# Dense work of a finished block, one turn of 16 tiles later in the three relation passes

## The chip, the cores and the metric
The kernel runs on one core of one Trainium2 chip. The metric is the device time of one execution in microseconds, without a profiler. The kernel before took 6027.67 us (median of 3 runs, 6023.32 to 6033.74).

## The reference
Four graph layers act on 5000 nodes with 128 features and 80,000 edges, sorted by target. Each layer normalises the rows (mean and variance over the features, then relu), computes a graph convolution and adds its result to the rows. The first is an attention layer, the second a weighted sum, the third three averaging convolutions. The change touches the fourth, which is three relational convolutions in a row (widths 128 to 256, 256 to 256, 256 to 128), with 8 kinds of edge:

```
seg = dst * 8 + etype
agg = segment_sum(x[src], seg)                 # one sum for each target and kind
mean = agg / maximum(count of seg, 1)
out = einsum('nrd,rdo->no', mean, W) + x @ root + b
h = relu(conv1(x)); h = relu(conv2(h)); out = conv3(h)
```

## The kernel before
Nodes lie in 40 blocks of 128, edges in 625 tiles of 128. A relational convolution is computed the other way round: first each node's row is multiplied with all 8 relation matrices and stored as a table with 8 rows per node; then a pass over the edges gathers for each edge the one row that belongs to its source and kind, weights it, and sums it into its target. The three edge passes are called p5, p6 and p7. While a pass sums, blocks of target nodes become finished one after the other, since edges are sorted by target. The dense work on a finished block (relu, the root product of the next convolution, the products for the next table, copies, the store) is placed between the tiles of the same pass. In p7 the dense work is only a transpose back to rows, the addition of the old rows and the store of the output.

An edge pass works like this. GpSimd gathers one tile after another with indirect DMAs into a ring of 16 slots (`gather`, L925 to L946). Before it fills a slot again, it waits for `mm_done`, which TensorE raises at the end of each quad of 4 tiles. TensorE (`tile`, L2354) multiplies each gathered tile with a selection matrix of 64 columns that VectorE makes; the four tiles of a quad add up in one PSUM bank, of which four are used in turn. VectorE (`quad`, L1781) makes a selection two quads ahead, waits for `mm_done`, adds the bank into the 64-column window of the accumulator, and raises `psum_free`, which frees the bank and also tells how many quads have been added.

Sixteen tiles, that is 4 quads, are a turn (`TURN`); a pass has 39 turns and one last tile. Each engine runs the same list of turns (`turns`, L415). Within a turn, `dense_step` (L426) puts one dense step behind each tile: the first four positions carry steps 12 to 15 of the block that was begun in the turn before, the other twelve carry steps 0 to 11 of the next block. Block b is begun at position 4 of turn b + 1. ScalarE begins it (step 0: `hidden`, L1304, or the copy at L1330): it waits until `psum_free` shows `added` quads, which is all quads up to the first one of the current turn. TensorE's root product is step 2, at position 6, and waits for ScalarE (`hid_made`). Its four table units are steps 4, 7, 10 and 13 in p5 (4 and 7 in p6), and ScalarE copies each from PSUM two steps behind, at 6, 9, 12 and 15, into a buffer that SyncE stores. In p7 TensorE's step 2 is the transpose (L2669) and VectorE's step 7 the sum with the old rows (L2217); SyncE stores the result and then loads the old rows of the block two further on into the buffer that has come free.

The engines' instruction lists are written out in this order; nothing is planned at run time. After the last turn and the last quad, `remaining` (L433) does what is left of the blocks: steps 12 to 15 of block 37, and blocks 38 and 39. The gather of the next pass waits until the tables of all 40 blocks have been stored.

Of the kernel before, what the change touches and what calls it, by code (L numbers as in the profile page):

```python
# [35 lines left out]
BLOCKS = -(-N // P)  # L36
# [14 lines left out]
TURN = 16  # L51
# [3 lines left out]
QUAD = 4  # L55
# [3 lines left out]
CREDIT = 4  # L59
TURNS = T // TURN  # L60
LAG = 2
SLACK = 4
SPAN = 16
SPANS = NP // SPAN
# [24 lines left out]
def build(nc, a, out):  # L89
    ctx = ExitStack()  # L90
    with ctx:
# [5 lines left out]
        def sem(name):  # L97
            if name not in made:
                made[name] = ctx.enter_context(nc.semaphore(name))
            return made[name]  # L100
# [263 lines left out]
        def chunks(p):  # L364
            return PASS[p]["F"] // P
# [37 lines left out]
        def later(i):  # L403
            return not isinstance(i, int) or i > 0
# [10 lines left out]
        def turns(eng, turn):  # L415

            turn(0, None, None, 0, 0)
            turn(1, None, (0, 0, 0), 0, 0)
            pairs = (TURNS - LAG) // 2
            with eng.Fori(0, pairs) as r:  # L420
                turn(2 * r + LAG, (2 * r, 0, r), (2 * r + 1, 1, r), 0, r)
                turn(2 * r + LAG + 1, (2 * r + 1, 1, r), (2 * r + 2, 0, r + 1), 1, r)
            for b in range(2 * pairs, TURNS - LAG):
                turn(b + LAG, (b, b % 2, b // 2), (b + 1, (b + 1) % 2, (b + 1) // 2), b % 2, b // 2)

        def dense_step(dense, j, k, last, first, added):  # L426

            if j < SLACK and last is not None:
                dense(TURN - SLACK + j, k, *last, added)
            if j >= SLACK and first is not None:  # L430
                dense(j - SLACK, k, *first, added)

        def remaining(step):  # L433

            for b in range(TURNS - LAG, BLOCKS):
                for j in range(TURN - SLACK if b == TURNS - LAG else 0, TURN):
                    step(j, b, b % 2, b // 2)

        def block_pairs(eng, body):
# [428 lines left out]
        def _(pool):  # L868
            pool.memset(X[:, (BLOCKS - 1) * P:NP], 0.0).then_inc(sem("x_padded"), 1)
            pool.memset(BASEF[:, :], float(N)).then_inc(sem("x_padded"), 1)  # L870
            pool.memset(HIGHF, 0.0).then_inc(sem("x_padded"), 1)
            pool.memset(TILEF[:, 0:SLACK], 0.0).then_inc(sem("x_padded"), 1)
            pool.iota(TILEF[:, SLACK:SLACK + TP - TURN].rearrange("o (g e) -> o g e", e=TURN), [[P, TP // TURN - 1], [0, TURN]], base=0, channel_multiplier=0,
# [158 lines left out]
        def _(act):  # L1032
# [31 lines left out]
            def dense_steps(p, dense):  # L1064

                with act.Fori(0, km) as k:
                    kq = act.snap((km * ORD[p] + k) * QUADS)

                    def spans(i, x):
                        v = SPAN_SLOT[x]  # L1070
                        span_out(act.snap(k * EARLY + PER_TURN * i + x), PER_TURN * i + x, v,
                                 act.snap(k * (TURNS * SLOT_USES[v]) + SLOT_USES[v] * i + x // 3))

                    def turn(i, last, first, u, r):
                        added = act.snap(kq + TURN // QUAD * i + (CREDIT + SLACK // QUAD))
                        for j in range(TURN):
                            dense_step(dense, j, k, last, first, added)
                            if p == 0 and j in SPAN_STEPS:
                                spans(i, SPAN_STEPS.index(j))

                    turns(act, turn)
                    added = act.snap(kq + QUADS + CREDIT)
                    remaining(lambda j, b, u, r: dense(j, k, b, u, r, added))

            def norm_root(n):

# [139 lines left out]
            for g in range(GROUPS):  # L1226
                u = g % 2
# [108 lines left out]
        def _(dve):  # L1336
# [204 lines left out]
            def rounds_reset(tag):  # L1541
                vec.memset(koff[:, :], 0.0).then_inc(sem("round"), 1)
# [221 lines left out]
            def sums(p, dense):  # L1764
                c = PASS[p]
                acc, C = c["acc"], chunks(p)
                rounds_reset(f"p{p}")
                with dve.Fori(0, km) as k:
                    kq = dve.snap((km * ORD[p] + k) * QUADS)
                    round_start(f"p{p}", k)  # L1770

                    def select(g, s):
                        there = iotaQ[:, :].unsqueeze(1).to_broadcast([P, QUAD, QWIN])
                        at = cols(QREL, g, QUAD).unsqueeze(2).to_broadcast([P, QUAD, QWIN])
                        hot = QHOT if c["degrees"] else QSEL
                        vec.tensor_tensor(hot[:, s, :, :], there, at, ALU.is_equal).then_inc(sem("s_hot"), 1)  # L1776
                        dve.wait_ge(sem("s_hot"), HOTS_OF[p] * km * (QUADS + AHEAD) + k * (QUADS + AHEAD) + g + 1)
                        vec.tensor_tensor(QSEL[:, s, :, :], hot[:, s, :, :], cols(c["wt"], g, QUAD).unsqueeze(2).to_broadcast([P, QUAD, QWIN]), ALU.mult) \
                            .then_inc(sem("s_ready"), 1)

                    def quad(g, s, first):  # L1781
                        select(g + AHEAD, (s + AHEAD) % 4)
                        dve.wait_ge(sem("mm_done"), kq + g + 2)
                        dve.wait_ge(sem("psum_free"), kq + g + CREDIT)
                        if c["degrees"]:
                            v = MULTI[:, bass.ds(first, QWIN)]
                            vec.tensor_tensor(v, v, PS[:, s, QWIN:2 * QWIN], ALU.add)
                        v = acc[:, 0:C, bass.ds(first, QWIN)]
                        vec.tensor_tensor(v, v, PS[:, s, 0:C * QWIN].rearrange("p (c w) -> p c w", w=QWIN), ALU.add).then_inc(sem("psum_free"), 1)  # L1789

                    def turn(i, last, first, u, r):
                        added = dve.snap(kq + TURN // QUAD * i + (CREDIT + SLACK // QUAD))
                        if p == 0:
                            dve.load(regs[0:8], TURN_AT[0:1, bass.ds(8 * i, 8)])
                            bases = [dve.snap(x, min_val=0, max_val=NP - QWIN) for x in regs[0:4]]
                            tiles = [dve.snap(x, min_val=0, max_val=T - 1) for x in regs[4:8]]
                        else:
                            bases = windows(dve, regs[0:4], QBASE[0:1, bass.ds(4 * i, 4)], QWIN)
                        for g in range(4):
                            if p == 0:  # L1800
                                span(dve.snap(k * EARLY + PER_TURN * i + g), PER_TURN * i + g, tiles[g], SPAN_SLOT[g])
                            quad(4 * i + g, g, bases[g])
                            for j in range(4 * g, 4 * g + 4):
                                dense_step(dense, j, k, last, first, added)
                    for g in range(AHEAD):
                        select(g, g)
                    turns(dve, turn)
                    last_bases = TURN_AT[0:1, bass.ds(8 * TURNS, 4)] if p == 0 else QBASE[0:1, bass.ds(QUADS - 1, 4)]
                    bases = windows(dve, regs[0:4], last_bases, QWIN)
                    quad(QUADS - 1, 0, bases[0])  # L1810
                    added = dve.snap(kq + QUADS + CREDIT)
                    dve.wait_ge(sem("psum_free"), added)
                    dve.sem_inc(sem("turn"), 1)
                    remaining(lambda j, b, u, r: dense(j, k, b, u, r, added))

            def sums_by_source():

# [404 lines left out]
        def _(pe):  # L2222
# [116 lines left out]
            def sums(p, dense):  # L2339
                c = PASS[p]  # L2340
                C = c["F"] // P
                with pe.Fori(0, km) as k:
                    kr = pe.snap(km * ORD[p] + k)
                    kq = pe.snap(kr * QUADS)
# [24 lines left out]
                            ins.then_inc(sem("mm_done"), 1)  # L2369

                    def turn(i, last, first, u, r):
                        added = pe.snap(kq + TURN // QUAD * i + (CREDIT + SLACK // QUAD))
                        for j in range(TURN):
                            slot = u * TURN + j if p == 0 else j
                            tile(4 * i + j // QUAD, j // QUAD, j % QUAD, slot, None if p == 0 and last is None else landed(slot, i if p else r), QUAD - 1,
                                 TURN * i + j if p == 0 and last is None else None)
                            dense_step(dense, j, k, last, first, added)
                            if p == 0 and j in SPAN_STEPS:
                                x = SPAN_STEPS.index(j)
                                span(pe.snap(k * EARLY + PER_TURN * i + x), SPAN_SLOT[x])  # L2380
                    turns(pe, turn)
                    if p == 0:
                        last = (T - 1) % FIRST_SLOTS
                        tile(QUADS - 1, 0, 0, last, landed(last, (T - 1) // FIRST_SLOTS - LAG * TURN // FIRST_SLOTS) - 16 * (QUAD - 1), 0)
                    else:
                        tile(QUADS - 1, 0, 0, 0, landed(0, TURNS) - 16, 0)
                    added = pe.snap(kq + QUADS + CREDIT)
                    remaining(lambda j, b, u, r: dense(j, k, b, u, r, added))

            def root(w, src, halves, kc, n, u):  # L2390

# [296 lines left out]
```

## Time and profile before

| | us |
|---|---|
| plain runs, median of 3 | 6027.67 |
| lowest, highest | 6023.32, 6033.74 |
| profiled execution, span | 6607.7 |
| TensorE busy in it | 4440.1 (67%) |
| GpSimd busy in it | 4113.5 (62%) |
| VectorE busy in it | 2723.9 (41%) |
| ScalarE busy in it | 1077.6 (16%) |

The profile was taken in an execution of its own; its length is known by its span, which is 580 us longer than the median of the plain runs. In a profile the engines are called PE (TensorE), PEld (its weight loads), DVE (VectorE), ACT (ScalarE), POOL (GpSimd) and SP (SyncE). L945 is line 945 of the kernel. The three relation passes fill the last 2823 us of the span. A float32 matmul shows as two records.

### The profile page before, as it was taken

How to read it: one execution, taken by the hardware profiler on the slowest of the kernel's cores; microseconds unless marked ns; L12 is line 12 of the kernel's file. 1: busy time of each engine (PE TensorE's matmuls, PEld its weight loads, DVE VectorE, ACT ScalarE, POOL GpSimd, SP SyncE). 2: the span in 40 equal slices, each digit the busy share in tenths (PEclk: the TensorE clock that was granted, in tenths of full speed). 3: DMA queues.
4: the chain of work that ended last, by engine and by line, in shares of the span. 5: the costliest groups of instructions: out<-in, count | busy, mean ns of one | idle time of the engine just before them, and what ended most of it. 6: DMA issues, size and time to landing. Idle time of an engine off the chain costs nothing.

```text
span 6607.7 us, 91944 instructions
## 1 busy us (share of the span) xinstructions
PE 4440.1 (67%) x24058; PEld 3442.2 (52%) x24058; DVE 2723.9 (41%) x8965; ACT 1077.6 (16%) x2081; POOL 4113.5 (62%) x3656
## 2 busy tenths in 40 slices
PE   2456676666666665999989977777766776533333
PEld 1344555544444444988876655555555555433333
DVE  7965555677777774322236411111111111111112
ACT  2521111122222222111113311111100000000000
POOL 2356666488888885744445466666566666566666
PEclk6566666666666666999999977888867666655555
DMA  6622222256555555744457734444333333211111
GB/s 158 210 71 77 76 77 76 67 100 102 99 98 100 99 100 153 221 146 131 125 177 255 255 121 132 133 130 133 122 109 114 110 111 109 75 52 50 52 50 50
DMA packets 569636, 764.26 MB, mean 116 GB/s; under 512 B 87625, under 2 KB 468064, under 8 KB 558608
## 3 DMA queue, kind: packets, MB, share of 16 engines
q1 hardware_dynamic: 327884, 422.38, 20.1%
q0 software_dynamic: 190256, 287.00, 20.1%
q10 hardware_dynamic: 51334, 52.94, 2.4%
q8 instruction: 75, 1.23, 0.1%
q14 instruction: 87, 0.71, 0.0%
HBM read 526.51 MB, written 235.79 MB: 115 GB/s over the span
## 4 chain that ended last, share of the span: by engine, by line
PE 32%; issue 17%; another core or an unknown queue 16%; DVE 11%; DMA 10%; POOL 9%; DVEq 3%; ACT 1%; ACTq 0%; POOLq 0%; SPq 0%
PE PS L2495 10%; DMA part<-ring,cur 8%; PE PS L2365 7%; POOL ring L945 5%; PE PS L2406 5%; POOL part L967 3%; DVE ACC_B L1755 2%; PE PS L2632 2%; PE PS L2396 2%; PE PS L2330 1%; DVE ACC_B L1753 1%; DVE QSEL L1776 1%; PE PS L2427 1%; PE PS L2572 1%
## 5 line engine op out<-in xcount | busy, mean ns | idle before, releaser
L2365 PE MATMUL PS<-QSEL,ring 128*128 128x64 f32 x7436 | 1393.7, 339 | 723.0 <-issue 327.9
L2365 PEld LDWEIGHTS PS<-QSEL,ring 128*128 128x128 f32 x7436 | 1354.3, 257 | 937.1 <-issue 671.3
L967 POOL DMA_INDIRECT part<-ring,cur x625 | 1010.0, 1616 | 250.9 <-issue 154.3
L945 POOL DMA_INDIRECT ring<-tab_l3b,SRC x625 | 599.7, 959 | 357.5 <-issue 208.6
L945 POOL DMA_INDIRECT ring<-tab_l3a,SRC x625 | 596.7, 955 | 359.0 <-issue 197.8
L945 POOL DMA_INDIRECT ring<-tab_l,SRC x593 | 587.9, 991 | 360.7 <-issue 160.8
L945 POOL DMA_INDIRECT ring<-tab_l3c,SRC x625 | 598.4, 957 | 326.0 <-issue 202.4
L2330 PE MATMUL PS<-ACC_B 128*128 128x320 f16 x2568 | 622.5, 410 | 116.2 <-issue 60.7
L1789 DVE TENSOR_TENSOR ACC_B<-ACC_B,PS 128x128 f32 (+1 forms) x314 | 79.7, 254 | 1429.1 <-remote 1006.6
L2406 PE MATMUL PS<-XM,SCR 128*128 128x512 f32 x960 | 580.7, 737 | 28.6 <-issue 14.5
L2427 PE MATMUL PS<-SCR,SEL 128*32 128x128 f32 x1250 | 275.2, 402 | 418.4 <-DVE SCR L1825 334.8
L1755 DVE TENSOR_SCALAR ACC_B<-ACC_B 128x640 f16<-128x640 f16 x1284 | 498.4, 450 | 0.0
L2330 PEld LDWEIGHTS PS<-ACC_B 128*128 128x128 f16 x2568 | 300.1, 127 | 359.0 <-issue 118.1
L2427 PEld LDWEIGHTS PS<-SCR,SEL 128*32 128x32 f32 x1250 | 188.7, 160 | 482.4 <-DVE SCR L1825 355.6
L1753 DVE TENSOR_SCALAR ACC_B<-ACC_B 128x128 f16<-128x128 f16 x1284 | 253.1, 287 | 339.2 <-PE PS L2330 257.9
L1789 DVE TENSOR_TENSOR ACC_A<-ACC_A,PS 128x64 f32 (+1 forms) x314 | 78.7, 251 | 726.7 <-remote 498.2
L1059 ACT CAST ACC_B<-PS 128x640 f16<-128x640 f32 x320 | 221.5, 692 | 586.7 <-PE PS L2330 334.0
L1112 ACT COPY SCR<-PS 128x512 f32<-128x512 f32 x240 | 138.2, 587 | 1095.8 <-remote 652.7
L2406 PEld LDWEIGHTS PS<-XM,SCR 128*128 128x128 f32 x960 | 204.1, 235 | 199.9 <-issue 182.2
L2040 DVE TENSOR_TENSOR SCR<-PS,ring 128x128 f32<-128x128 f32 (+1 forms) x120 | 40.2, 335 | 586.6 <-PE PS L2495 571.2
L2495 PE MATMUL PS<-ACC_exact,slots_exact 128*128 128x512 f32 x1070 | 263.8, 397 | 0.0
L1776 DVE TENSOR_TENSOR QSEL<-iotaQ,QREL 128x256 f32<-128x256 f32 x477 | 201.5, 422 | 87.2 <-issue 86.2
(494 smaller groups left out, 6767.0 us busy)
## 6 DMA issues: line engine op xcount, KB each, us to landing
ring<-pairs_d SPq DMA_DIRECT2D x60, 1280.0 KB
pairs_d<-ACC_B ACTq DMA_DIRECT2D x320, 160.0 KB
SCR<-pairs_d SPq DMA_DIRECT2D x40, 1280.0 KB
SCR<-in_src SPq DMA_DIRECT2D x128, 320.0 KB
tab_l3a<-SCR SPq DMA_DIRECT2D x40, 1024.0 KB, 4.4
tab_l3b<-SCR SPq DMA_DIRECT2D x40, 1024.0 KB
ACC_A<-pairs_d SPq DMA_DIRECT2D x20, 1280.0 KB
tab_l3c<-SCR SPq DMA_DIRECT2D x40, 512.0 KB
```

Of the source, the lines that this page charges most:

```text
L945: pool.indirect_dma_start(gathered(p, slot), None, tab[p][:, :], bass.IndirectOffsetOnAxis(SRC[:, t:t + 1], 0)).then_inc(sem(f"pair_in{slo ...
L967: pool.indirect_dma_start(part_d[m][:, :], bass.IndirectOffsetOnAxis(cur[:, s:s + 1], 0), ring[:, s, 0:D], None, compute_op=ALU.add).then_ ...
L1059: nc.scalar.copy(SPAN_OUT[:, v, :].rearrange("p (h c) -> p h c", h=2), PS[:, 6:8, 0:SPAN_COLS // 2]).then_inc(sem("span_out"), 1)
L1753: vec.tensor_scalar(LOWS[:, v, e, :], iota_low, LOW[:, bass.ds(tile + e, 1)], None, ALU.is_equal)
L1755: ins = vec.tensor_scalar(PAIRS[:, v, e, :], iota_pairs, KEY[:, bass.ds(tile + e, 1)], OFFS[:, bass.ds(at, 1)], ALU.subtract, ALU.is_equal)
L1776: vec.tensor_tensor(hot[:, s, :, :], there, at, ALU.is_equal).then_inc(sem("s_hot"), 1)
L1789: vec.tensor_tensor(v, v, PS[:, s, 0:C * QWIN].rearrange("p (c w) -> p c w", w=QWIN), ALU.add).then_inc(sem("psum_free"), 1)
L2330: ins = mm(PS[:, 6 + h, 0:SPAN_COLS // 2], LOWS[:, v, e, :], PAIRS[:, v, e, h * (SPAN_COLS // 2):(h + 1) * (SPAN_COLS // 2)], start=e == 0 ...
L2365: ins = mm(PS[:, s, ch * QWIN:(ch + 1) * QWIN], rows, hot, start=e == 0 and ch == 0, stop=e == end, skip_group_check=True)
L2406: ins = mm(PS[:, 6 + m % 2, :], part_hid[:, u, ch, :], relw[:, at:at + 512], start=ch == 0, stop=ch == kc - 1)
L2427: ins = mm(windows_out[0:WIN, j * P:(j + 1) * P], SEL[:, j, :], same[:, j, :], start=True, stop=True)
L2495: ins = mm(to if conv == 1 else to.rearrange("p (k n) -> p k n", k=2), slot[:, e * P:(e + 1) * P], conv_source(conv, h), start=h == 0, sto ...
```

## The change
In the passes p5, p6 and p7 (wherever `p` is not 0) block b is begun at position 4 of turn b + 2 and no longer of turn b + 1. The number of quads that are waited for stays the one from before: `added_by` takes one turn of quads off. So the block waits for quads that were added a turn earlier. The first dense work stands in turn 2, and `remaining` begins one block earlier, with steps 12 to 15 of block 36 and then blocks 37, 38 and 39. The pass p0 keeps its order. Ring, buffers, banks and instructions of a step are the same; 39 - 3 turns are an even number, so the turn that was written out behind the loop is gone and one more is written out ahead of it.

```diff
+LATE_LAG = 3
...
+        def late_turns(eng, turn):
+
+            turn(0, None, None, 0, 0)
+            turn(1, None, None, 0, 0)
+            turn(2, None, (0, 0, 0), 0, 0)
+            pairs = (TURNS - LATE_LAG) // 2
+            with eng.Fori(0, pairs) as r:
+                turn(2 * r + LATE_LAG, (2 * r, 0, r), (2 * r + 1, 1, r), 0, r)
+                turn(2 * r + LATE_LAG + 1, (2 * r + 1, 1, r), (2 * r + 2, 0, r + 1), 1, r)
+
+        def pass_turns(p, eng, turn):
+            (late_turns if p else turns)(eng, turn)
+
+        def added_by(p, i):
+
+            return TURN // QUAD * (i - (1 if p and later(i) else 0)) + (CREDIT + SLACK // QUAD)
...
-        def remaining(step):
-
-            for b in range(TURNS - LAG, BLOCKS):
-                for j in range(TURN - SLACK if b == TURNS - LAG else 0, TURN):
+        def remaining(p, step):
+
+            lag = LATE_LAG if p else LAG
+            for b in range(TURNS - lag, BLOCKS):
+                for j in range(TURN - SLACK if b == TURNS - lag else 0, TURN):
                     step(j, b, b % 2, b // 2)
...
-                        added = act.snap(kq + TURN // QUAD * i + (CREDIT + SLACK // QUAD))
+                        added = act.snap(kq + added_by(p, i))
...
-                    turns(act, turn)
+                    pass_turns(p, act, turn)
...
-                    remaining(lambda j, b, u, r: dense(j, k, b, u, r, added))
+                    remaining(p, lambda j, b, u, r: dense(j, k, b, u, r, added))
```
VectorE's and TensorE's lists (`sums`) are changed in the same three places.

## Rows read from the trace of the kernel before

**Rows 1.** Busy time by engine, granted clock, DMA share: windows of p5, p6, p7.
```profile
3785.00:4751.00 966.00, 747.98 (x3460) 537.85 (x3460) 167.80 (x479) 131.70 (x280) 596.43 (x625) 0.81 0.41 130
4751.00:5696.00 945.00, 651.89 (x2980) 526.35 (x2980) 166.46 (x479) 78.16 (x160) 599.90 (x626) 0.68 0.36 110
5696.00:6608.00 912.00, 335.41 (x1290) 289.53 (x1290) 167.35 (x509) 11.80 (x40) 598.11 (x625) 0.50 0.19 51
```

**Rows 2.** Line 945, the gathers: ns least/median/most, first and last start.
```profile
L945 POOL DMA_INDIRECT ring<-tab_l3a,SRC x625: 943/949/1167, 3784.7 to 4714.8; - x157
L945 POOL DMA_INDIRECT ring<-tab_l3b,SRC x625: 943/949/1196, 4751.0 to 5672.0; - x157
L945 POOL DMA_INDIRECT ring<-tab_l3c,SRC x625: 942/947/1202, 5695.8 to 6596.3; - x157
L945 POOL DMA_INDIRECT ring<-tab_l,SRC x593: 942/947/1809, 323.7 to 1270.8; - x198
```

**Rows 3.** Timeline of GpSimd in p7: start, length, idle before it and releaser.
```profile
6026.78 0.95 POOL L945 DMA_INDIRECT ring<-tab_l3c,SRC  x1 [0.31 <-issue]
```

**Rows 4.** Waits in p5: us in total, times, longest.
```profile
ACT SCR L1112 <- remote: 268.0, 43, 13.6
...
PE PS L2396 <- ACT SCR L1306: 87.9, 26, 10.1
```

**Rows 5.** Waits in p6.
```profile
PE PS L2396 <- ACT SCR L1306: 29.9, 22, 8.7
```

**Rows 6.** Waits in p7.
```profile
PE PS L2669 <- ACT SCR L1330: 172.0, 15, 13.6
```

**Rows 7.** Timelines of TensorE, VectorE, ScalarE and GpSimd around one stop in p7.
```profile
6023.10 1.11 PE L2365 MATMUL PS<-QSEL,ring 128*128 128x64 f32 x4 [1.25 <-DMA ring<-tab_l3c,SRC]
...
6028.14 0.69 PE L2365 MATMUL PS<-QSEL,ring 128*128 128x64 f32 x2 [1.25 <-DMA ring<-tab_l3c,SRC]
6042.35 0.47 PE L2669 MATMUL PS<-ident,SCR 128*128 128x128 f32 x1 [13.52 <-ACT SCR L1330]
...
6041.45 0.22 DVE L1789 TENSOR_TENSOR ACC_B<-ACC_B,PS 128x64 f32 x1 [7.07 <-remote]
...
6041.92 0.30 ACT L1330 COPY SCR<-ACC_B 128x128 f32 x1 [35.85 <-DVE ACC_B L1789]
...
6042.03 0.94 POOL L945 DMA_INDIRECT ring<-tab_l3c,SRC  x1 [4.33 <-remote]
```

**Rows 8.** Timeline of TensorE in p5: one unit product, then three tiles.
```profile
4024.43 1.94 PE L2406 MATMUL PS<-XM,SCR 128*128 128x512 f32 x4
4026.21 1.45 PE L2365 MATMUL PS<-QSEL,ring 128*128 128x64 f32 x12
```

**Rows 9.** Timeline of TensorE at the end of p5.
```profile
4726.98 1.16 PE L2396 MATMUL PS<-SCR,root 128*128 128x128 f32 x8 [0.99 <-ACT SCR L1306]
4727.97 7.03 PE L2406 MATMUL PS<-XM,SCR 128*128 128x512 f32 x16
4735.99 1.16 PE L2396 MATMUL PS<-SCR,root 128*128 128x128 f32 x8 [0.99 <-ACT SCR L1306]
```

**Rows 10.** Timeline of TensorE at the end of p6.
```profile
5671.12 3.18 PE L2406 MATMUL PS<-XM,SCR 128*128 128x512 f32 x4
...
5681.88 0.71 PE L2396 MATMUL PS<-SCR,root 128*128 128x128 f32 x4 [2.34 <-ACT SCR L1306]
...
5687.02 0.71 PE L2396 MATMUL PS<-SCR,root 128*128 128x128 f32 x4 [0.99 <-ACT SCR L1306]
```

**Rows 11.** End of p7, by engine; then a DMA row (KB each, us to landing).
```profile
6604.20 0.50 ACT L1330 COPY SCR<-ACC_B 128x128 f32<-128x128 f32 x2 [15.74 <-DVE ACC_B L1789]
...
6605.41 0.50 DVE L2217 TENSOR_TENSOR SCR<-PS,SCR 128x128 f32<-128x128 f32 x2 [1.31 <-PE PS L2669]
...
6606.19 0.32 SPq L853 DMA_DIRECT2D out<-SCR  x1
...
SCR<-x_l SPq DMA_DIRECT2D x80, 64.0 KB, 2.0
```

More of the change, by code:

```diff
@@ L1791, in turn @@
                     def turn(i, last, first, u, r):
-                        added = dve.snap(kq + TURN // QUAD * i + (CREDIT + SLACK // QUAD))
+                        added = dve.snap(kq + added_by(p, i))
                         if p == 0:
@@ L1806, in sums @@
                         select(g, g)
-                    turns(dve, turn)
+                    pass_turns(p, dve, turn)
                     last_bases = TURN_AT[0:1, bass.ds(8 * TURNS, 4)] if p == 0 else QBASE[0:1, bass.ds(QUADS - 1, 4)]
@@ L1813, in sums @@
                     dve.sem_inc(sem("turn"), 1)
-                    remaining(lambda j, b, u, r: dense(j, k, b, u, r, added))
+                    remaining(p, lambda j, b, u, r: dense(j, k, b, u, r, added))
             def sums_by_source():
@@ L2371, in turn @@
                     def turn(i, last, first, u, r):
-                        added = pe.snap(kq + TURN // QUAD * i + (CREDIT + SLACK // QUAD))
+                        added = pe.snap(kq + added_by(p, i))
                         for j in range(TURN):
@@ L2380, in turn @@
                                 span(pe.snap(k * EARLY + PER_TURN * i + x), SPAN_SLOT[x])
-                    turns(pe, turn)
+                    pass_turns(p, pe, turn)
                     if p == 0:
@@ L2387, in sums @@
                     added = pe.snap(kq + QUADS + CREDIT)
-                    remaining(lambda j, b, u, r: dense(j, k, b, u, r, added))
+                    remaining(p, lambda j, b, u, r: dense(j, k, b, u, r, added))
             def root(w, src, halves, kc, n, u):
```

## The prediction
> **What bounds the kernel now.** I began with the spans of the four stages that gather by edge. The three relation passes (p5, p6, p7) are the windows of [rows 1]: 966, 945 and 912 us, 2823 of the profiled 6607.7. Next, what sets their pace. GpSimd gathers 625 tiles per pass, one start every 1.25 us when nothing holds it (0.95 us and 0.30 of issue, [rows 3]), and its busy time is the same 596 to 600 us in each pass, while TensorE's falls from 748 to 335. The first and the last gather [rows 2] stand 930.1, 921.0 and 900.5 us apart; 624 starts at 1.25 us are 780. So GpSimd is the pace setter and has lost 150, 141 and 120 us to full ring slots, 411 in all; the first edge pass of the kernel the same way lost 947.1 - 592 x 1.25 = 207. All four: 618 us.
>
> Next, the wait that the change aims at. TensorE's root product (or p7's transpose) for a block waits until ScalarE has read the block, and ScalarE waits until VectorE has added the first quad of the current turn. TensorE has only three tiles between that quad and the product. It lost 87.9 us in 26 waits in p5, 29.9 in p6, 172.0 in p7 [rows 4 to 6]: 290 us. The question is whether GpSimd, and not only TensorE, gets any of it back.
>
> One such stop in p7 answers it [rows 7]. TensorE ran the last tiles of the turn's first quad at 6023.1 and tile 6 at 6028.1, then waited 13.5 us. VectorE added that quad only at 6041.45, ScalarE copied at 6041.92, TensorE went on at 6042.35. GpSimd, which wanted a slot, went on at 6042.03: before TensorE did. So its release was a quad finished before the stop, whose signal came about 17 us late, and with it VectorE, ScalarE, GpSimd and TensorE all got up within a microsecond. The stop is an effect of the late signal beside GpSimd's wait; taking it away doesn't make the signal earlier.
>
> The Trainium skill, Perfetto Trace Analysis, section Tensor Engine Instruction, says that a matmul's end in a profile is estimated from its size and that the semaphore goes out only when PSUM has acknowledged the write. The trace agrees as far as it goes: the modelled end of that quad is near 6024.2 and its reader started at 6041.45. If the products truly ended that late, the late signal is part of the work and no order of dense steps moves it; the sum would stay as below.
>
> **Profile against the clock on the wall.** The profiled span is 6607.7 us, the median of the plain runs 6027.67: 580 us less. That is nearly the 618 us that the gathers lost. My reading: most late signals belong to the profiled execution, and plain runs gather close to 1.25 us per tile, with some 38 us of losses over four passes, about 25 of them in p5 to p7 (411/618). This assumes that the other stages are the same in both; if they too are stretched, more than 25 is left here.
>
> Would the wait exist without late signals? From VectorE's add to TensorE's restart is 0.90 us (6041.45 to 6042.35, [rows 7]). Three tiles of p5 are 1.45 us of TensorE at the fast clock [rows 8], and at the gather's pace they are 3.75 us. So with a prompt signal TensorE doesn't stop, or by a few tenths. Nor is TensorE the pace setter in p5: a turn is 16 tiles at 1.45/3 = 7.7 us, four units at 1.94 = 7.8 and a root at 1.16, together 16.7 of the 20.0 us that 16 gathers take.
>
> **The change, part by part.**
> Dense steps one turn later, same quads awaited: nothing is added or removed inside a turn; each turn carries one block's root, units, copies and table store as before. Gain bounds: below, 0; above, all of p5 to p7's losses, 411 us in the profile and about 25 in a plain run. Even in the profile the wait does not wholly go in p5 and p6: ScalarE works in order, and before it reads block b it has to copy unit 3 of block b-1, whose product is signalled by TensorE too; those copies waited 268.0 us in p5, up to 13.6 at a time [rows 4]. A late signal then holds ScalarE at the copy and TensorE at the root as before. I take 1 to 2 us of gain in a plain run, nearest to the prompt case.
>
> Turns 0 and 1 now have no dense work, turn 2 has the first twelve steps: 16.7 us of TensorE work where GpSimd sets the pace: 0. The turn written out at the end goes and one at the start comes; one more register operation per turn: 0, hidden under the gather of four quads; no row shows it, and the nearest, VectorE's shortest add of 0.22 us [rows 7], would make 39 x 0.22 = 9 us a pass if nothing covered it, but VectorE is busy 168 of 966 us [rows 1].
>
> The tail is the certain cost. After the last quad, blocks 37 to 39 are now to be done in full (and the last four steps of 36), instead of 38 and 39 and four steps of 37. Nothing hides this: the next pass's gather starts only when the whole table is stored, 36.2 us after the last gather of p5 and 23.8 after that of p6 [rows 2], and p7's end is the kernel's end.
> - p5: in the tail a block takes from root to root 4735.99 - 4726.98 = 9.0 us, of which 7.03 is its unit products, the rest root and the wait for ScalarE [rows 9]. One block more: 9.0.
> - p6: 5687.02 - 5681.88 = 5.1 us [rows 10].
> - p7: a transpose, an add, a store. Block 39's old rows are loaded only after block 37's sum is done, and that is now in the tail: the load takes about 2.0 us (the like load of 64 KB), where the last adds were 0.5 us for two [rows 11]. Last copies 6604.20, block 37's sum by about 6605.4 (the two sums start at 6605.41, [rows 11]; one sum is half of their 0.50), load issued about 0.7 later, landed 6608.1, sum and store issue 6608.7 against 6606.5 before: 2.2. Bounds 0.3 (load no limit) and 4.
> Stores: SyncE has one more table store in the tail per pass, but it is waited for only at the end and overlaps the next block's 9.0 or 5.1 us, and buffers come back in time (they alternate).
> Sum: 9.0 + 5.1 + 2.2 = 16.3, less 1.5 of gain: +15. On the profiled execution 6607.7 + 15 = 6623; on the median 6027.67 + 15 = 6043. Bounds of the tail: where TensorE runs at its 1.2 GHz level, four records of unit product take 3.18 us and not 1.8 [rows 10], so a p5 block is 4 x 3.18 + 2 x 1.16 + 1 = 16, a p6 block 2 x 3.18 + 2.2 = 8.6; with p7's 4: 29. Least: if the last turn loses its own wait (2 us in each of two passes, an estimate from p6's 29.9/22 = 1.4 a wait): 12.
>
> **Rivals.**
> A. The waits reach the gathers in plain runs too. For: 290 us of TensorE waits, and TensorE stopped keeps ring slots full. Against: GpSimd's restart before TensorE's. If the profile's extra 580 us (8.8% of the span) lay evenly over all stages, p5 to p7 would still lose 411 - 0.088 x 2823 = 163 us plainly; half of it back is -81, with the tail -65: 5963. It decides from 28 us given back (16.3 + 12).
> B. Given back about what the tail costs: half of the 25 us, 12.5, and the rest from last-turn waits: +2, 6030.
> C. The tail at the slow clock: +29, 6057. For: the granted clock falls from 0.81 to 0.68 and 0.50 over the passes [rows 1]. Against: both tails ran their products at the fast level in the profile [rows 9, 10].
> D. The clock gives something back. With fewer stops TensorE stays at 2.4 GHz longer; the granted clock in p5 is 0.81, p7 is at 0.50 with its 172 us of waits. p7 and p6 have TensorE to spare, so only p5 could gain: if the slow share makes turns longer than 20.0 us, up to its 150 us of losses in the profile, 6 to 9 in a plain run (150/618 of 38): 6043 - 9 = 6034.
> The Trainium skill, TensorE: Matmul & The Clock Gate, section HAM oscillation, says that a loop which makes TensorE wait between short groups of matmuls drops to the slow clock again and again, and it would speak for this change as for D; the trace bears it out only in that the clock is lowest where TensorE is least busy, and there GpSimd sets the pace.
> That the change doesn't remove the wait (ScalarE's copies hold it, or the quad awaited is still the late one) gives the forecast's time, with the tail paid.
>
> **How the numbers follow.** Forecast 0.48 (6043, own range 6036 to 6050), C 0.08, B and D together 0.26, A 0.18. No change means within 12 us (0.2%), about what a measurement of this kernel can tell. Slower by over that: most of the forecast (0.44) and C, 0.52. Same: B, D and the low end of the forecast, 0.29. Faster: A with a rest of D, 0.19. The range reaches from 6008, into A's upper part, to 6058, C's time.
>
> **What would show it.** In the changed profile: the gap from the last gather of p5 to the first of p6 grows from 36.2 to about 45 us, from p6 to p7 from 23.8 to about 29; one root group and its units more after the last tile; TensorE's waits in p7 on ScalarE's copy nearly gone; those in p5 less reduced. GpSimd's distance from first to last gather stays within some 20 us of 930, 921 and 901. I am wrong if these distances shrink by more than 28 us together in plain terms, that is, if the time comes out under 6015.

## The result and the profile after

The changed kernel took 6048.38 us (median of 6, 6044.60 to 6051.95) against 6026.58 for the kernel before beside it (6023.32 to 6034.38): ratio 1.0031, 95% interval 1.0021 to 1.0041, so 19 us slower by the ratio and 22 by the medians. In two later series of runs it was 1.0021 (1.0012 to 1.0030) and 1.0022 (1.0013 to 1.0032), that is +13 and +14 us. The forecast was +15. (A series is a set of runs of several kernels, the kernel before always among them, on one chip.)

One thing has to be said before any rows are compared: the series fell into two groups, and in one, the short group, the kernel before takes 6016 to 6027 us, in the other, the long group, 6566 to 6609. The profile ahead of the prediction (6607.7 us) is from the long group, the one of the changed kernel (6042.9 us) from the short one. Read side by side they would say that the change saves 565 us. Only profiles of one group may be compared, so the kernel before was profiled again; that profile, of the short group, is `before_third` (6007.9 us).

Line 964 of the changed kernel, all gathers: least, median and most ns, first and last start in us. It answers to [rows 2].

```profile
L964 POOL DMA_INDIRECT ring<-tab_l3a,SRC x625: 942/947/1202, 3601.7 to 4390.5; - x157
L964 POOL DMA_INDIRECT ring<-tab_l3b,SRC x625: 942/947/1202, 4432.7 to 5222.8; - x157
L964 POOL DMA_INDIRECT ring<-tab_l3c,SRC x625: 939/945/1142, 5250.7 to 6032.6; - x157
L964 POOL DMA_INDIRECT ring<-tab_l,SRC x593: 940/947/1814, 320.2 to 1115.5; - x198
```

The same view of the kernel before in `before_third`.

```profile
L945 POOL DMA_INDIRECT ring<-tab_l3a,SRC x625: 942/946/1191, 3588.5 to 4373.8; - x157
L945 POOL DMA_INDIRECT ring<-tab_l3b,SRC x625: 942/946/1196, 4407.6 to 5196.0; - x157
L945 POOL DMA_INDIRECT ring<-tab_l3c,SRC x625: 940/944/1196, 5219.2 to 6000.1; - x157
L945 POOL DMA_INDIRECT ring<-tab_l,SRC x593: 940/944/1818, 319.1 to 1112.9; - x198
```

Subtract within a line, and from line to line:

| us | before | changed | difference | forecast |
|---|---|---|---|---|
| p5, first to last gather | 785.3 | 788.8 | +3.5 | 0 |
| last of p5 to first of p6 | 33.8 | 42.2 | +8.4 | +9.0 |
| p6, first to last gather | 788.4 | 790.1 | +1.7 | 0 |
| last of p6 to first of p7 | 23.2 | 27.9 | +4.7 | +5.1 |
| p7, first to last gather | 780.9 | 781.9 | +1.0 | 0 |
| last of p7 to the end of the span | 7.8 | 10.3 | +2.5 | +2.2 |

The three tails (what is left after the last gather of a pass) make +15.6 where 16.3 was forecast. A pass is 780 us of gathers at one per 1.25, and the distances are 1 to 10 us longer than that, with or without the change. The two spans differ by more, 35 us, since p0 and the unchanged stages around it were 13 us longer in this execution, 11 of them between p0 and p5. The other three profiles of the short group (`changed_again`, `only_p6`, `only_p7`) are 4 to 9 us longer there too than `before_third`, which is its only profile of the kernel before; why is not shown. A second profile of the changed kernel (`changed_again`, 6037.3) has gaps of 42.7, 27.6 and 10.2 and distances of 786.7, 789.4 and 781.2: 16.1 in the tails, and 2.7 in place of 6.2 inside the passes, so that much of the latter is scatter of single executions.

The tail of p5 in the changed kernel, TensorE's timeline (start, length, what, idle before it and who ended it); it answers to [rows 9].

```profile
4399.67 1.16 PE L2415 MATMUL PS<-SCR,root 128*128 128x128 f32 x8 [0.99 <-ACT SCR L1325]
4400.66 7.03 PE L2425 MATMUL PS<-XM,SCR 128*128 128x512 f32 x16
4408.69 1.16 PE L2415 MATMUL PS<-SCR,root 128*128 128x128 f32 x8 [0.99 <-ACT SCR L1325]
...
4417.71 1.16 PE L2415 MATMUL PS<-SCR,root 128*128 128x128 f32 x8 [0.99 <-ACT SCR L1325]
4418.70 7.03 PE L2425 MATMUL PS<-XM,SCR 128*128 128x512 f32 x16
```

Three roots, 9.02 us apart, where [rows 9] have two: blocks 37, 38, 39. And the end of p7, VectorE's last sums and SyncE's last transfers; it answers to [rows 11].

```profile
6038.16 0.67 DVE L2236 TENSOR_TENSOR SCR<-PS,SCR 128x128 f32<-128x128 f32 x2 [1.31 <-PE PS L2688]
6040.99 0.29 DVE L2236 TENSOR_TENSOR SCR<-PS,SCR 128x128 f32<-128x128 f32 x1 [2.16 <-DMA SCR<-x_l2r]
...
6038.63 0.35 SPq L874 DMA_DIRECT2D out<-SCR  x1
6039.19 0.34 SPq L661 DMA_DIRECT2D SCR<-x_l2r  x1
6039.84 0.35 SPq L874 DMA_DIRECT2D out<-SCR  x1
6041.31 0.32 SPq L872 DMA_DIRECT2D out<-SCR  x1
```

The sum of block 39 waits 2.16 us for the old rows, whose load (L661, issued at 6039.19) stands behind block 37's store (6038.63).

Where was the wait that the change removes? These are TensorE's waits on ScalarE in `before_third`, over the whole execution, and then in the changed kernel (us in total, times, longest).

```profile
PE PS L2396 <- ACT SCR L1306: 5.3, 4, 2.3
PE PS L2669 <- ACT SCR L1330: 1.2, 1, 1.2
```
```profile
PE PS L2415 <- ACT SCR L1325: 7.3, 6, 2.4
PE PS L2688 <- ACT SCR L1349: 1.4, 1, 1.4
```

In the short group the kernel before has no such wait to lose: 6.5 us in 120 blocks, not the 290 us of [rows 4 to 6], and these too stand in the tails, as the changed kernel's 8.7 do.

### The profile page after: what moved, and what is told of

Its sections match the earlier page's. It is cut to its first block, busy times and chain, and to the rows that moved or that the text cites. A ratio compares the mean times of both kernels' runs of the same rounds, so it can differ in the third digit from the quotient of the medians.

```text
span 6042.9 us, 91938 instructions
## 1 busy us (share of the span) xinstructions
PE 4397.2 (73%) x24058; PEld 3392.6 (56%) x24058; DVE 2731.2 (45%) x8965; ACT 1076.2 (18%) x2081; POOL 4110.3 (68%) x3656
## 4 chain that ended last, share of the span: by engine, by line
POOL 27%; PE 26%; DMA 20%; issue 18%; DVE 6%; ACT 1%; DVEq 1%; POOLq 0%; SPq 0%; ACTq 0%
POOL ring L964 23%; DMA part<-ring,cur 11%; PE PS L2514 11%; PE PS L2384 5%; DMA ring<-tab_l3c,SRC 4%; POOL part L986 4%; PE PS L2425 3%; PE PS L2651 2%; DMA ring<-tab_l3a,SRC 2%; DMA ring<-tab_l3b,SRC 1%; PE PS L2415 1%; PE PS L2591 1%; PE PS L2593 1%; PE PS L2604 1%; DVE ACC_B L1774 0%
## 5 line engine op out<-in xcount | busy, mean ns | idle before, releaser
L2384 PE MATMUL PS<-QSEL,ring 128*128 128x64 f32 x7436 | 1442.7, 347 | 778.6 <-DMA ring<-tab_l3c,SRC 354.2
L2349 PE MATMUL PS<-ACC_B 128*128 128x320 f16 x2568 | 594.8, 396 | 68.1 <-DVE ACC_B L1774 67.6
L2425 PE MATMUL PS<-XM,SCR 128*128 128x512 f32 x960 | 550.0, 704 | 0.0
L2059 DVE TENSOR_TENSOR SCR<-PS,ring 128x128 f32<-128x128 f32 (+1 forms) x120 | 40.2, 335 | 584.8 <-PE PS L2514 569.3
```

The lines of the kernel that those rows point to most:

```text
L2349: ins = mm(PS[:, 6 + h, 0:SPAN_COLS // 2], LOWS[:, v, e, :], PAIRS[:, v, e, h * (SPAN_COLS // 2):(h + 1) * (SPAN_COLS // 2)], start=e == 0 ...
L2384: ins = mm(PS[:, s, ch * QWIN:(ch + 1) * QWIN], rows, hot, start=e == 0 and ch == 0, stop=e == end, skip_group_check=True)
L2425: ins = mm(PS[:, 6 + m % 2, :], part_hid[:, u, ch, :], relw[:, at:at + 512], start=ch == 0, stop=ch == kc - 1)
```

## The experiments

All ratios are to the kernel before in the same series. The four series of this section ran on chips 5, 1, 6 and 5, in this order; the second is of the short group, the others are of the long one. The kernels with a later order in some passes come from the changed kernel, with a lag for each pass in place of `LATE_LAG`. They were built from it with

```diff
-            return TURN // QUAD * (i - (1 if p and later(i) else 0)) + (CREDIT + SLACK // QUAD)
+            lag = LAGS.get(p, LAG)
+            return TURN // QUAD * (i - (lag - LAG if not isinstance(i, int) or i >= lag - 1 else 0)) + (CREDIT + SLACK // QUAD)
...
-            lag = LATE_LAG if p else LAG
+            lag = LAG if p in CATCH_UP else LAGS.get(p, LAG)
```

`LAGS` has a number for each pass: with 2 block b is begun at turn b + 1, with 3 at turn b + 2.

**before_again** (chip 5): the kernel before, unchanged.

> The kernel before, profiled once more, to have a profile as long as its plain runs. Theory T (the change costs the tail alone: one more block of dense work after the last quad of each relation pass; the wait it removes was worth nothing): first to last gather 780 to 792 us in p5, p6 and p7, as in the changed kernel's profile (788.8, 790.1, 781.9), and TensorE's waits on ScalarE before its root product a few us in a pass in place of 88, 30 and 172; gaps between passes about 33 and 20 us. Rival W (the waits did hold the gathers up in plain runs, and the gain is hidden by a larger loss): first to last gather longer than the changed kernel's by 5 us or more in a pass, and waits of 20 us or more. Time 6027 by both.

6605.35 us (6599.19 to 6625.17), beside runs of the kernel before of 6608.53. These are plain runs, with no profiler, and they are as long as the profile of before. That ended the prediction's reading that the late signals belong to the profiled execution. All three distances (934.7, 923.6, 905.5) are far above the 780 to 792 that T expected, but those were numbers of the short group, so nothing was told on T and W.

**before_third** (chip 1): the same in another series.

> The kernel before, for its profile. On a chip where it takes 6027 us T expects distances of 780 to 792 us in each pass, gaps of 33 and 20 to 23 us, and TensorE's waits on ScalarE's relu and copy under 10 us in a pass; W expects distances 5 us longer than the changed kernel's. On a chip where it takes 6608 it repeats the profile there is, and shows how far two profiles of one kernel differ.

6016.13 us (ratio 0.9998). Its rows stand above: distances 785.3, 788.4, 780.9, waits of 5.3 and 1.2. T's numbers, with gaps of 33.8 and 23.2. W expected the kernel before to gather more slowly; it does not. But here it has no wait to remove, so this says nothing of what a removed wait is worth.

**lag4** (chip 5): block b begun at turn b + 3.

```diff
-LATE_LAG = 3
...
+        LAGS = {5: 4, 6: 4, 7: 4}
```

> Block b is begun at turn b + 3, for the same quads: two blocks more than before are left for each tail. T: the price doubles, 2 x 19 to 2 x 22 over before: 6065 to 6071. P: more than that, as the order costs in every turn. If the measured +22 of the change were an accident of code placement or of the clock, no doubling: 6045 to 6055.

6642.78 against 6608.53: ratio 1.0056 (1.0042 to 1.0069), +37 us by the ratio (28 to 46), where T expected +38 to +44. That is twice the price of the change, 13 to 19 us in its three series: no accident, and P's "more than that" is not seen. The gaps are 51.3 and 36.4 against 36.5 and 26.7 in `before_again`, less than two blocks each (18 and 10 us) would add; the table behind `early_relu` shows why. The distances are 932.3, 921.2, 899.8 against 934.7, 923.6, 905.5.

**only_p5, only_p5_2, only_p6, only_p7** (chips 5, 6, 1, 1): the later order in one pass.

```diff
-LATE_LAG = 3
...
+        LAGS = {5: 3, 6: 2, 7: 2}     # only_p6: {5: 2, 6: 3, 7: 2}; only_p7: {5: 2, 6: 2, 7: 3}
```

> The later order in p5 alone; p6 and p7 as before. T: the block of p5's tail costs 9.0 us: 6036, gap from p5 to p6 9 us longer than before, that from p6 to p7 unchanged. W: under 6030. P: 6040 or more.

> The later order in p5 alone, again. T: +9, gap from p5 to p6 42.7 us, the other two as before (23.2, 7.8). P: +14 or more, as on the slower chip (+16, interval 9 to 22).

> The later order in p6 alone. T: the tail's block of p6: +5 to +8 (the 8 where the block runs at TensorE's slow level). P: +12 or more.

> The later order in p7 alone, where the wait removed was the largest (190 us of TensorE on the chip of 6608 us). T: +2, the load of block 39's old rows; within 0.1% of before. W: -10 or more, most of all here.

p5 alone: 1.0024 (1.0014 to 1.0034) and 1.0014 (1.0005 to 1.0023), +16 and +9. The first alone speaks for P, the second is T's number; the mean, 12, is between T's 9 and P's 14, and the two intervals together don't exclude either. The gap from p5 to p6 is 46.6 and 42.2 (42.7 was expected), that from p6 to p7 30.9 and 23.4, where the kernel before has 36.2 to 36.5 and 23.8 to 26.7. p6 alone: 1.0009 (1.0000 to 1.0018), +5. p7 alone: 1.0005 (0.9996 to 1.0014), +3, T's number, and not W's -10; but it ran in the short group, where p7 has 1.2 us of the wait and not 190, so it could not test W. In the profiles of the short group each edit moves its own gap: p6 alone 23.2 to 27.8 with p5's at 33.9; p7 alone the end from 7.8 to 10.3 with 33.9 and 23.5 before it. Each part's effect is near what can be told by times; the unchanged gaps of this group repeat within 0.3 us.

**catch_up, catch_up_2** (chips 5, 6): the later order with the tail of the kernel before, so the removed wait alone.

```diff
+        LAGS = {5: 3, 6: 3, 7: 3}
+        CATCH_UP = (5, 6, 7)
...
+            upto = TURNS - 6 if p in CATCH_UP else TURNS
...
+            if p in CATCH_UP:
+                steps = [(b, j) for b in range(upto - lag, TURNS - LAG + 1) for j in range(TURN)][TURN - SLACK:-SLACK]
+                for i in range(upto, TURNS):
+                    at = [(16 * (i - upto) + j) * len(steps) // 96 for j in range(TURN + 1)]
+                    turn(i, None, [steps[at[j]:at[j + 1]] for j in range(TURN)], 0, 0)
```

> The changed kernel's turns (block b begun at turn b + 2) up to turn 32; in the last six turns 112 dense steps stand on the 96 positions, so that the tail is again that of the kernel before (steps 12 to 15 of block 37, blocks 38 and 39). T: the same as before within 4 us, 6027, gaps between passes as before. W: the removed wait shows without the tail's price: under 6020. Rival P (the later order costs something inside the turns as well): 6032 or more, the gathers' distances longer than in the kernel before.

> The kernel with the later order and the tail of the kernel before, again. On a chip where the kernel before takes about 6020 us, T: within 5 us of it, gaps 33.8 and 23.2 us and 7.8 after the last gather, as in the kernel before; the +6.6 us of the slower chip (interval 0 to 13) was chance or TensorE's extra steps in the last turns. P: +6 or more again.

Ratios 1.0010 (1.0000 to 1.0020) and 0.9995 (0.9986 to 1.0004), that is +7 and -3 us: the first lies where P expected it, the second does not, and together there is no difference that can be told. Both are of the long group, where the wait is real: TensorE's waits on ScalarE in p7 were 189.9 us in `before_again`, 12.3 in `catch_up` and 2.1 in `catch_up_2`. W wanted under 6020 in a 6027 kernel, that is -7 us or more; the second interval reaches to -9, so a gain of a few us is not excluded, one of 10 is. The gaps were 35.9, 29.0 and 9.1, then 40.2, 28.6 and 10.1; the 33.8, 23.2 and 7.8 that were expected are of the short group. The tails hold two blocks, as in the kernel before; why the 40.2 is long is in the table behind `early_relu`.

**changed_again, changed_third** (chips 1, 5): the changed kernel.

> The changed kernel once more, beside the kernel before and on the same chip. If the chip is one where the kernel before takes some 6608 us: T: +16 to +22, the gathers' distances within 8 us of 934.7, 923.6 and 905.5 although TensorE's waits on ScalarE fall from 136 (p5 and p6) and 190 us (p7) to under 60 and under 15; gap from p5 to p6 46, from p6 to p7 30 us. W: distances shorter by 10 us or more in a pass. If it is one where the kernel before takes 6027: +19 again, gaps 42 and 28.

> The changed kernel a third time. If the chip is one where the kernel before takes over 6550 us: the distances between first and last gather as in the kernel before there (922 to 935, 912 to 924, 894 to 906), TensorE's waits on ScalarE in p7 under 15 us where the kernel before has 172 to 190, and the time +15 to +22, the tails' price. If the removed wait were worth something where signals come late, it would be +5 or less. On a chip of about 6020 us: +13 to +19 as before.

6036.93 against 6020.62 (ratio 1.0021), +13 us where +19 was expected, with gaps of 42.7 and 27.6 (42 and 28 expected), and 6580.35 against 6565.95 (1.0022), +14 us where +15 to +22 was expected. The last is the test of the wait, in the group where it exists. First the waits of the kernel before in `before_again` (whole execution), then of `changed_third`.

```profile
POOL ring L945 <- remote: 530.5, 185, 5.8
PE PS L2669 <- ACT SCR L1330: 189.9, 18, 13.8
PE PS L2396 <- ACT SCR L1306: 135.4, 48, 9.6
PE PS L2365 <- DVE ACC_B L1789: 69.8, 10, 7.3
```
```profile
POOL ring L964 <- remote: 477.0, 166, 5.7
PE PS L2384 <- DVE ACC_B L1808: 138.0, 23, 8.7
PE PS L2384 <- DVE QSEL L1797: 67.4, 27, 8.2
PE PS L2415 <- ACT SCR L1325: 62.8, 18, 11.4
PE PS L2688 <- ACT SCR L1349: 2.9, 1, 2.9
```

Of 325 us of TensorE's waits on ScalarE 66 are left. But TensorE does not stop 260 us less. Its tiles wait 138.0 us for VectorE's add, which frees a bank, in place of 69.8, and 67.4 us for VectorE's selections in place of 8.9: 127 us of the stop have moved to the next things that hang on the same late add, and the waits for gathered tiles grow by 91 us. GpSimd's waits on full slots, in which p0 has its share, barely moved. The distances, `changed_third`:

```profile
L964 POOL DMA_INDIRECT ring<-tab_l3a,SRC x625: 941/949/1193, 3768.4 to 4687.5; - x157
L964 POOL DMA_INDIRECT ring<-tab_l3b,SRC x625: 941/949/1205, 4737.2 to 5648.3; - x157
L964 POOL DMA_INDIRECT ring<-tab_l3c,SRC x625: 938/947/1201, 5679.2 to 6572.1; - x157
```

That is 919.1, 911.1 and 892.9. Each is 1 to 3 us under the range that was expected. The nearest profile with the order of before is `early_relu` (below, its kernel before at 6571.64): 923.1, 913.7 and 894.9. So at most 9 us came back in three passes, from 260 us of waits on ScalarE. The tails were dearer there: gaps of 49.7 and 30.9, and 13.4 at the end, against 31.7 + 2, 26.3 and 7.8 in `early_relu` (2 us is what its edit was expected to save): +26, of which 7.8 is the first part of the table behind `early_relu`. Together +17, where +14 was measured.

VectorE's adds in p7 of `changed_third`, with no stop of TensorE behind ScalarE left:

```profile
5800.18 0.22 DVE L1808 TENSOR_TENSOR ACC_B<-ACC_B,PS 128x64 f32 x1 [2.63 <-issue]
...
5816.42 0.22 DVE L1808 TENSOR_TENSOR ACC_B<-ACC_B,PS 128x64 f32 x1 [15.11 <-issue]
...
5826.94 0.22 DVE L1808 TENSOR_TENSOR ACC_B<-ACC_B,PS 128x64 f32 x1 [9.40 <-remote]
...
5828.49 0.21 DVE L1808 TENSOR_TENSOR ACC_B<-ACC_B,PS 128x64 f32 x1
```

and the same adds of the kernel before in `before_third`:

```profile
5802.11 0.22 DVE L1789 TENSOR_TENSOR ACC_B<-ACC_B,PS 128x64 f32 x1 [3.34 <-PE PS L2365]
...
5807.08 0.22 DVE L1789 TENSOR_TENSOR ACC_B<-ACC_B,PS 128x64 f32 x1 [3.15 <-PE PS L2365]
...
5812.18 0.22 DVE L1789 TENSOR_TENSOR ACC_B<-ACC_B,PS 128x64 f32 x1 [3.97 <-PE PS L2365]
```

In the short group a quad's add comes every 5.0 us, as its four gathers do. In the long one adds come now and then 16.2 and 10.5 us behind the one before, and the next follows after 1.6 us; [rows 7] have such a late add in the kernel before, and here it happens with no stop behind ScalarE. So the late signal is the cause and the stop its effect.

**early_relu** (chip 6): the kernel before, with one edit in ScalarE's tail.

```diff
-                    remaining(lambda j, b, u, r: dense(j, k, b, u, r, added))
+                    order = []
+                    remaining(lambda j, b, u, r: order.append((j, b, u, r)))
+                    if p in (5, 6):
+                        last = 15 if p == 5 else 9
+                        for b in (BLOCKS - 2, BLOCKS - 1):
+                            begin = next(x for x in order if x[:2] == (0, b))
+                            order.remove(begin)
+                            order.insert(next((n for n, x in enumerate(order) if x[:2] == (last, b - 1)), 0), begin)
+                    for j, b, u, r in order:
+                        dense(j, k, b, u, r, added)
```

> The kernel before, with ScalarE's order in the tails of p5 and p6 alone changed: it reads blocks 38 and 39 before it copies the last unit of the block ahead, so that TensorE's root products need not wait 0.99 us each behind that copy. If the tail is TensorE's chain, as T has it, the gap from p5 to p6 falls by 1 to 2 us (33.8 to 32 or 33) and that from p6 to p7 by 1 to 2 (23.2 to 22); the time by 2 to 4 us, which is less than can be told. If the copies or the stores set the tail, the gaps stay.

Ratio 0.9998 (0.9989 to 1.0007): not to be told from before, as expected. TensorE's timeline at the end of its p5:

```profile
4689.63 1.16 PE L2405 MATMUL PS<-SCR,root 128*128 128x128 f32 x8 [0.44 <-ACT SCR L1315]
4690.63 7.03 PE L2415 MATMUL PS<-XM,SCR 128*128 128x512 f32 x16
4697.50 1.05 PE L2405 MATMUL PS<-SCR,root 128*128 128x128 f32 x8
4698.39 7.03 PE L2415 MATMUL PS<-XM,SCR 128*128 128x512 f32 x16
```

The waits of 0.99 us are 0.44 and 0, and from root to root it is 7.9 us in place of 9.0: the edit saves 1.7 us, within the 1 to 2 expected, so p5's tail is TensorE's chain. The gap to p6, 31.7 us, is 4.5 us and more under the 36.2 to 36.5 of the kernel before in the long group; the rest of that is not the edit, as the table shows. In p6 the expected fall doesn't show: the gap is 26.3 where the kernel before has 23.2 to 26.7. The second root product there doesn't wait either, but the first tail block's products ran near TensorE's slow level (6.16 us for 8 records, 3.60 at the fast one). No version tried beats the kernel before by an amount that can be told.

**What a tail of p5 is made of.** The start times of TensorE's root products split every gap into three parts.

| us | last gather to first root of the tail | from root to root | last root to first gather of p6 | gap |
|---|---|---|---|---|
| `before_third`, short group | 9.8 | 9.0 | 15.0 | 33.8 |
| changed kernel, short group | 9.2 | 9.0, 9.0 | 15.0 | 42.2 |
| kernel before, [rows 2, 9] | 12.2 | 9.0 | 15.0 | 36.2 |
| `before_again` | 12.5 | 9.0 | 15.0 | 36.5 |
| `catch_up` | 11.9 | 9.0 | 15.0 | 35.9 |
| `catch_up_2` | 16.2 | 9.0 | 15.0 | 40.2 |
| `only_p5` | 13.5 | 9.0, 9.0 | 15.0 | 46.6 |
| `only_p5_2` | 9.1 | 9.0, 9.0 | 15.0 | 42.2 |
| `changed_third` | 16.7 | 9.0, 9.0 | 15.0 | 49.7 |
| `lag4` | 9.2 | 9.0, 9.0, 9.0 | 15.0 | 51.3 |
| `early_relu` | 8.9 | 7.9 | 14.9 | 31.7 |

The block that the change adds is 9.0 us in every profile, and `lag4` has two. What scatters is the first part, by up to 7.8 us in the long group: how far TensorE is behind when the last gather goes out. In `changed_third` it had just waited 10.4 us for ScalarE there. In p6 the added block is 5.1 us each time (5.14), and what scatters besides the first part is the tail's first block, 5.1 to 8.2 us by the clock that it gets.

## Why the prediction was right, and where it was not

- **GpSimd sets the pace, and gets nothing from TensorE's removed wait.** Right within what can be told, and tested where the wait exists: 260 us less waiting of TensorE on ScalarE, 9 us in the gathers' distances, which is inside what two profiles of one kernel differ by (`before` and `before_again`: 930.1, 921.0, 900.5 against 934.7, 923.6, 905.5, 12 us in all). Against the profile ahead of the prediction `changed_third`'s distances are 28.5 us shorter, which touches the limit of 28 set there, but its series is shorter for the kernel before too (6565.95 us, where that profile spans 6607.7). What the prediction did not see: half of the stop does not go but moves to TensorE's waits on VectorE, which hang on the same late signal.
- **The tail.** Right term by term: 9.0, 5.1, 2.2 forecast; in the short group the gaps grew by 8.4 to 8.9, 4.4 to 4.7, 2.4 to 2.5, and from root to root the added blocks are 9.0 and 5.1. In the long group the gaps scatter too much to read a block from them (+5.7 to +13.5 in p5), but from root to root it is the same 9.0 and 5.1. p7's 2.2 rested on block 39's load coming behind block 37's store, and its row shows it.
- **Profile against the clock on the wall.** This step was wrong. I read the 580 us between profile and plain runs as the profiler's. `before_again`'s plain runs take 6605 us. The late signals go with the chip or the condition that a series ran in, and come with and without a profile. The conclusion drawn, that plain runs at 6027 gather at 1.25 us and hold no wait, was right for the short group for another reason: `before_third` shows no late signals there at all. That part was luck. The forecast did not hang on it: in the long group, where the wait is real, the change costs +14 as well, which is what the row with GpSimd's restart ahead of TensorE's said alone.
- **The wait does not wholly go in p5 and p6.** Right: in `changed_third` 62.8 us are left of 135.4, in p7 2.9 of 189.9.
- **Gain of 1 to 2 us inside the turns.** In the short group none: the distances are 6 and 3 us longer in the two profiles. In the long group it is not to be told from the scatter of 12 us. The forecast +15 is the tails' 16.3 less this 1.5; the three series measured +19, +13 and +14.
- **Rivals.** A (the waits reach the gathers in plain runs) fell with `catch_up`, `catch_up_2` and `changed_third`. C (tail at the slow clock) priced four records at the slow level at 3.18 us, but that group ran only in part at it: at the slow level they take 3.73 (TensorE in `changed_again`, at 5213.42). It happened in one block: in the changed kernel's p6 the first tail block took 7.9 us (roots at 5228.91 and 5236.85), the other 5.1; but in `before_third` the first tail block is as slow (5202.37 to 5210.50), so the block that the change adds ran at the fast level and took 5.1 (the gap grew by 4.7). D: in the long group the granted clock of p5, p6 and p7 is 0.80, 0.68 and 0.50 in `before_again` and 0.80, 0.69 and 0.50 in `changed_third`; removing the waits on ScalarE gave the clock nothing. The Trainium skill, TensorE: Matmul & The Clock Gate, section HAM oscillation, describes waits that keep the clock low; here the engine is at its 1.2 GHz level in p7 with 189.9 us of those waits or with 2.9. Its work there comes in pieces of 1.1 us about every 2.5.

## What to carry to other kernels

A wait is worth removing only if the engine that sets the pace was waiting for it; look for who gets up first when it ends, and here the pace setter got up before the engine that was to be freed. When a wait shrinks, add up all waits of that engine: the stop may only have moved. Work begun later in a software pipeline costs one more step of it in the drain, and with three passes the drain is paid three times: it can be read from two start times of the profile of before. Before a profile is used for or against plain runs, compare its span with them, and when they differ by 10%, time the kernel again before saying why. Where a gap scatters from profile to profile, split it at the starts of its own work: the part that was changed may repeat to 0.02 us while the rest moves by 8.

## What the runs showed of the hardware

The same kernel takes 6016 to 6027 us in some series and 6566 to 6609 in others. In the latter TensorE's signals reach the other engines up to 17 us late in the edge passes: first to last gather 785 us in p5 became 919 to 935, and 793 to 796 us in p0 became 933 to 954. The waits tell the groups apart at once: a releaser called `remote` stands in every profile of the long group (530.5 us of GpSimd's waits in `before_again`) and in none of the five of the short one. The series whose chip is on record ran on chip 1 (short) and on chips 5, 6 and 5 (long), so the group may go with the chip; with one short series among four that is not shown, and chip 5 alone gave 6608.53 and 6565.95 for the kernel before. Memory placement and neighbours were not tried, and why a finished matmul's signal comes in bunches stays open. Also open is whether p5 alone costs more than its block of 9.0 us: it measured 16 us in one series and 9 in another. The 4.4 us between the gaps of the two profiles are all in the part ahead of the tail's first root, but the rest is not explained.
